# Routing steps of all but the last batch row counted as ready later in the model of the order, and the third routing done two rows at a time

## The reference, cut to what matters

```python
x = _layernorm(x + _L1_ffn_ref(x, ...))   #  8 experts, each token takes 1
x = _layernorm(x + _L2_ffn_ref(x, ...))   # 16 experts, each token takes 2
x = _layernorm(x + _L3_ffn_ref(x, ...))   # 31 experts, each token takes 3, and a shared one
# router of the third:
aff = softmax(x @ Wr + br); vals, idx = top_k(aff, 3)
gates = sum(one_hot(idx, 31) * vals[..., None], axis=-2)
```

## Time and profile before

| What | us |
| --- | --- |
| median of 3 runs | 2488.06 (2477.15 to 2500.33) |
| profiled execution, its own time | 2486.54 |
| span of the profiled execution | 2484.6 |
| around the span (difference of the two) | 1.94 |
| PE busy | 2100.0 (85%) |
| DVE busy | 1537.5 (62%) |
| ACT busy | 1161.9 (47%) |
| POOL busy | 607.7 (24%) |

### The profile page before, as it was taken

One profiled execution on the slowest core, in us unless ns is written; L12 is line 12 of the kernel. 1 busy time (PEld: TensorE's weight loads), 2 busy tenths in 40 slices (PEclk: granted clock), 3 DMA queues, 4 the chain that ended last, 5 costly groups with the idle time before them and its releaser, 6 DMA issues. The chain is left out here.

```text
span 2484.6 us, 44836 instructions
## 1 busy us (share of the span) xinstructions
PE 2100.0 (85%) x15577; PEld 1056.6 (43%) x15608; DVE 1537.5 (62%) x3533; ACT 1161.9 (47%) x2248; POOL 607.7 (24%) x951
## 2 busy tenths in 40 slices
PE   4799999997799999886999999888596998788482
PEld 1133355443323334473555444443494344334362
DVE  5678766657888855546566655545366776447445
ACT  1377765572167765231465566662143443151141
POOL 4102102113421102243121111214241000215563
PEclk8799999898889999986898989888797999898696
DMA  4500111110101100071111000100492000100374
GB/s 147 191 27 27 28 40 31 29 30 1 49 16 30 41 18 17 14 250 54 37 32 34 23 22 12 34 22 27 161 342 78 1 1 1 45 17 27 87 196 146
DMA packets 135676, 148.34 MB, mean 60 GB/s; under 512 B 30033, under 2 KB 120593, under 8 KB 134174
## 3 DMA queue, kind: packets, MB, share of 16 engines
q1 hardware_dynamic: 97374, 100.77, 13.7%
q10 hardware_dynamic: 30272, 28.60, 3.6%
q0 software_dynamic: 7808, 16.10, 1.8%
HBM read 72.42 MB, written 26.99 MB: 40 GB/s over the span
## 5 line engine op out<-in xcount | busy, mean ns | idle before, releaser
L1896 DVE TENSOR_REDUCE maxima<-psM 128x2 f32<-128x1024 f32 (+4 forms) x640 | 678.1, 1081 | 349.0 <-PE psM L1544 131.1
L1755 ACT ACTIVATE probs<-psE 128x512 f32<-128x512 f32 (+2 forms) x1248 | 699.6, 584 | 408.1 <-PE psE L1567 190.9
L1567 PE MATMUL psE<-q_stack,k_stack 53*128 53x512 bf16 (+3 forms) x1152 | 372.1, 360 | 44.5 <-ACT probs L1755 35.1
L1544 PE MATMUL psM<-k_stack,q_stack 51*128 51x512 bf16 (+3 forms) x1280 | 353.4, 351 | 9.2 <-DVE maxima L1896 5.9
L1567 PEld LDWEIGHTS psE<-q_stack,k_stack 53*128 53x128 bf16 x1152 | 98.0, 94 | 242.1 <-ACT probs L1755 155.3
L2464 POOL DMA_INDIRECT by_token<-probs,y_slot x148 | 141.7, 958 | 130.2 <-DVE probs L2408 113.8
L1544 PEld LDWEIGHTS psM<-k_stack,q_stack 51*128 51x128 bf16 x1280 | 102.7, 98 | 165.4 <-issue 89.4
L1474 PE MATMUL psM<-masks_bf,ident_bf 64*128 64x128 bf16 (+2 forms) x832 | 156.1, 270 | 5.2 <-DMA k_stack<-k_parts 5.1
L1474 PE MATMUL psE<-masks_bf,ident_bf 64*128 64x128 bf16 (+2 forms) x960 | 156.2, 248 | 0.0
L2082 POOL TENSOR_SCALAR pool_t<-mean_var 128x4 f32<-128x4 f32 x60 | 14.9, 248 | 576.4 <-DVE mean_var L1820 572.5
L1587 PE MATMUL psB<-probs,values 128*32 128x256 f32 (+3 forms) x1728 | 154.3, 429 | 1.4 <-ACT probs L1755 0.9
(11 more groups left out here) (508 smaller groups left out, 3736.4 us busy)
## 6 DMA issues: line engine op xcount, KB each, us to landing
q_stack<-q_parts SPq DMA_DIRECT2D x432, 64.0 KB
values<-experts_dram SPq DMA_DIRECT2D x40, 514.0 KB, 4.9
q_stack<-experts_dram SPq DMA_DIRECT2D x79, 128.5 KB, 3.2
k_stack<-k_parts SPq DMA_DIRECT2D x156, 64.0 KB
probs<-sorted ACTq DMA_DIRECT2D x148, 65.0 KB, 4.6
hid<-experts_dram SPq DMA_DIRECT2D x15, 514.0 KB, 4.8
work<-experts_dram SPq DMA_DIRECT2D x15, 514.0 KB, 4.8
sorted<-hid ACTq DMA_DIRECT2D x7, 1024.0 KB, 10.7
```

What stands on the lines that cost most here:

```text
L1544: out, len(heads), keys, lo, max_mask(c, t), lambda i, to, start, stop: nc.tensor.matmul(to, q_stack[lo:lo + R_MAX, job.a % Q_SLOTS, pair_ ...
L1567: lambda h, to, start, stop: nc.tensor.matmul(to, ks[lo:lo + R_END, pairs[h], k * P:k * P + c.kn], q_stack[lo:lo + R_END, job.a % Q_SLOTS, ...
L1755: nc.scalar.activation(probs[0:c.kn, m % 2, heads[0]:heads[-1] + 1, q0:S], psE[0:c.kn, n % 2, 0:len(heads) * (S - q0)].rearrange("p (h q) ...
L1896: nc.vector.tensor_reduce(top, psM[:, at:at + len(banks), 0:per * keys].rearrange("p b (h k) -> p b h k", h=per), AX_X, ALU.max, negate=Tr ...
```

## The change

A tuple `LATER` names nine kinds of routing items, and in `count()` each of them may start, in the model, no sooner than 3.0 us after what it needs has ended; the last routing of a segment is left out of this. The number acts in all three segments. It is a number in the model only: no wait is added to the program. And the third router's span goes from 1 to 2, so rows 0 and 1 are routed together, and rows 2 and 3.

```diff
@@ -150,6 +150,8 @@
 OPENS = ("q", "k", "v", "rq", "rk", "rows", "gather", "turn", "out", "back", "hidden", "logits", "ranks")
+LATER = ("logits", "pick_a", "soft", "pick_b", "ranks", "slots", "pages", "label", "scatter")
+SLACK = 3.0
@@ -687,6 +689,8 @@  (in count(), ready())
             if item[0] == "root" and self.roots.get((item[1], item[2])) != rooted:
                 return None
+            if item[0] in LATER and item[1] is not self.routes[-1]:
+                at += SLACK
@@ -2729,7 +2733,7 @@
-        to1, to2, to3 = Routing(1, E1, K1, 1, False), Routing(2, E2, K2, 1, False), Routing(3, E3 - 1, K3, 1, True)
+        to1, to2, to3 = Routing(1, E1, K1, 1, False), Routing(2, E2, K2, 1, False), Routing(3, E3 - 1, K3, 2, True)
```

## The result

| | before | changed |
| --- | --- | --- |
| median of 4 runs, us | 2485.78 (2477.15 to 2500.33) | 2546.19 (2534.64 to 2552.41) |
| profiled execution, us | 2486.54 | 2552.41 |
| span of it, us | 2484.6 | 2550.6 |

The ratio is 1.0215, 95% interval 1.0178 to 1.0252: 53 us slower (44 to 63) on 2485.78. The two medians of the table stand 60 us apart. 2531 was predicted, with 2502 to 2552 as the range and 80% for slower.

What follows compares the result with a forecast made beforehand. The prediction took row 3's chain of attention, layernorm, logits and routing to set each segment's end, with executed fills holding it up; 31 + 12 + 2 = 45 us on 2486.54 gave 2531, range 2502 to 2552.

Steps and rivals of the forecast that it cites:

- What the 3 us become: All segments: the model writes longer idle time out as 176 more executed fills, 39 us of PE time.
- the three terms: Predicted changes of the three segments' lengths: +31, +12 and +2 us.
- Segment 1, (a): Up to row 3's `rows`: `split` ends earlier, at 1002, but 35 fills make `rows` 1.3 us later.
- Segment 1, (b): From `rows` to `post_a`: 22.0 us kept to the third `share`, plus 10.3; `post_a` 14.2 us later.
- rival C: The new long runs meet PE's low clock, 0.50 instead of 0.22 us for some 100 fills: +28, 2560; 7%.
- Segment 1, (c): From `post_a` to row 3's `slots`: 73 fills take 16.3 us, `slots` at 1081.0 against 1049.53, +31 us.
- Rival A's +8: Segment 1, fills only cover: row 2's routing behind row 3's `post_b` costs 8.2 us; the rival had 8%.
- Segment 2: `rows` 10 us and `post_a` about 4.5 earlier, then 44 and 82 fills make the tail 30.9: net +12.
- rival D: Fills hold PE's clock at full in three stretches and give 13 us back: 2518; 14%.
- Segment 3: Pairs end `pages` near 2305 instead of 2319.7, but 24 scatters follow the barrier: +2.
- Rival B: Only the last runs (73, 82, 92) bind; those among the shares hide beneath exponentials: +24, 2510; 14%.

Runs made afterwards that it cites:

- e1: The change with its 3 us alone, the third routing row by row as before: 2582.01 us, ratio to before 1.0383.
- e4: The kernel before with 100 more fills directly ahead of row 3's last ranks in segments 1 and 2 each: 2534.67 us, ratio 1.0212.
- e5: The change without its three last runs of fills (73, 82 and 92): 2528.51 us, ratio to before 1.0146.
- e3: The change without its seven long runs of fills (35, 35, 73, 44, 82, 55, 92): 2524.85 us, ratio to before 1.0166.
- e7: The change with 30 fills instead of 9 ahead of row 3's exponentials in segment 1: one run, 2543.98 us.
- e2: The change with the pairs alone, the added lateness set to 0: 2493.29 us, ratio to before 1.0022.
- e8: The kernel before with 3 instead of 17 fills between rows and row 3's exponentials in segment 1: one run, 2504.88 us.
- e9: The kernel before with 20 instead of 3 fills between rows and row 3's exponentials in segment 2: ratio 0.9998.

## Why the prediction was right, and where its sizes were off

- **What the 3 us become: right.** They are executed as fills, and these hold up what stands behind them (e1, e4, e5). The places were the ones named: run of 35, run of 73 and 82 with DVE idle for 7.93 and 7.55 us behind `pick_b`; 7 had been said for the first. They are not the whole loss: with the seven long runs taken out, 34 of the 55 us of the segments stayed, at a lower clock (e3).
- **The sum was helped by luck.** 45 us were said (its terms are 46 before they were rounded down) and 55 came by the segments, but the three terms missed by +12.7, -5.1 and +2.4, so errors of opposite sign took part of each other back.
- **Segment 1, (a):** `rows` 4.4 us later instead of 1.3. `split` ended at 1003.5 (1014.80 less 11.3), 1.5 us behind the 1002 said, and the run took 9.19 instead of 7.8 us, as its first part met the lower clock.
- **Segment 1, (b): the term that was mis-sized.** The 22.0 us from `rows` to the third `share` were carried over as if the clock stayed, and 10.3 added. It took 41.8, where 32.3 were predicted: PE's part from the first exponential step to `ranks` 25.1 us instead of 16.5 (1029.87 to 1054.95, before 1013.95 to 1030.46), and the second run 9.57 instead of 7.8. In e7 the same part takes 16.2 us (1033.87 to 1050.10) at 1.00, so the 8.6 are the clock's. The prediction's rival C saw that the lower clock could cost, but put the price on the fills; most of it fell on the matmuls between them.
- **Segment 1, (c): the right size, with half of it put on the wrong cause.** 28.4 us from `post_a` to the last `slots`, 29.6 predicted. Taking out the run of 73 gives back 6.8 (e3) to 7.4 us (e5) of its excess of 16.0, and DVE's order keeps the other 8.6 to 9.2. The prediction put the whole on the fills ("Its cover being gone is the whole of this term"); yet by its own `pick_b`, which was to end near 1074 and wait 7 us, only those 7 were the run's. Rival A's +8 was there, beneath.
- **Segment 2:** +6.9 for +12. The tail was 29.8 for 30.9; `post_a` came 8.5 us sooner, not 4.5. `rows` came 7.4 sooner, where 10 was said, and from `rows` to `post_a` it took 1.1 less, where 5.6 more was said. The clock of 1.00 for 0.71 and 0.61 goes with the second figure, but is not shown to be all of it: the same list as before took 29.0 us there in e2, at a clock of 0.76, against 32.1 before and 31.0 in the change. So rival D's clock came in segment 2 and its opposite in segment 1; its 14% were given to one sign for all segments.
- **Segment 3:** +4.4 for +2. The widths cost 0.42 and 0.93 us (0.42 and 0.94 said); less the offset of 62.1 the last `pages` end at 2305.3 (2305 said) and the first pair's scatters at 2306.8 (2306). The barrier let POOL go 4.06 us after its last scatter, not 1.8 us, and that is the difference. The 1.8 had been read where DVE's `pages` came last at the barrier; now POOL's scatters did.
- **Rival B falls for segment 1:** the second run did not hide beneath exponentials, which were over when it began. What it cost beyond DVE's order is not measured: in e3, without it, the third `share` waited for row 1's `slots` instead, and the clock was lower.

What stood ahead of row 3's exponentials goes with their clock, with one exception. Where it was 1.00, 17 fills stood there in one piece (before in segment 1, the change in segment 2) or 3 and 30 (e7). Where it fell, 3 and 9 stood there with a pause between them (the change in segment 1), or 3 (e8, and before in segment 2). Before, in segment 1:

```profile
1010.27 3.84 PE L1597 MATMUL psB<-masks_bf,ident_bf 128*128 128x512 bf16 x16 [0.67 <-ACT max_rows L1764]
```

The exception is e9: 20 in one piece, with `back` and the logits of another row between them and the exponentials, and the clock fell all the same. Why is left open.

## What to carry to other kernels

A number that exists only in a scheduler's model becomes real where the model writes its idle time out as work; look there first for what a change of the model will execute. Dummy work is free while it is no longer than the work that it stands beside, and past that costs its full length; but in places it also pays for PE's clock in what follows, so a run must be judged together with the stretch behind it, not matmul by matmul. And when a wider step halves the work of one engine, look at what it gathers behind the next barrier.

## What the runs showed of the hardware that was not expected

Fourteen 128x512 dummy matmuls (3.1 us) less ahead of a stretch made that stretch 14 us longer (e8), and 21 more made another 6.6 us shorter (e7): the lower level lasts on over work in which PE is busy throughout (21.00 of 21 us at 0.50). In the change the clock fell although PE had paused for no longer than 0.68 us in the 13 us before. Two executions of the same instructions differed by 6 us in one stretch, at a clock of 0.91 and 0.70. Where POOL came last at the third barrier it passed it 4.06 and 3.97 us (e2) after its last scatter; before, where DVE came last, POOL passed it 1.8 us after DVE's end.
